# Causal attention on Trainium2: the diagonal mask added by VectorE in place of two identity products on TensorE

## What is computed

```python
q = (x @ Wq).reshape(b, t, HKV, G, HD)
k = (x @ Wk).reshape(b, t, HKV, HD)
v = (x @ Wv).reshape(b, t, HKV, HD)
scores = jnp.einsum('bqhgd,bkhd->bhgqk', q, k) / jnp.sqrt(jnp.float32(HD))
causal = jnp.tril(jnp.ones((t, t), bool))
scores = jnp.where(causal, scores, NEG)
attn = jax.nn.softmax(scores, axis=-1)
ctx = jnp.einsum('bhgqk,bkhd->bqhgd', attn, v).reshape(b, t, HQ * HD)
return ctx @ Wo
```

## Time and profile before

| what | value |
|---|---|
| median of 3 runs | 1102.44 us (1102.1, 1102.44, 1114.94) |
| the profiled execution's own time | 1114.54 us |
| its span, first to last instruction | 1112.8 us |
| mean granted TensorE clock | 0.901 |
| busy over the span: TensorE / weight load / VectorE / ScalarE / GpSimd | 87% / 45% / 70% / 56% / 41% |
| causal attention, items 0 to 127 | from 566 to about 900 us |

### The profile page before, as it was taken

One profiled execution on the slowest core, in us unless ns is written; L12 is line 12 of the kernel. 1 busy time (PEld: TensorE's weight loads), 2 busy tenths in 40 slices (PEclk: granted clock), 3 DMA queues, 4 the chain that ended last, 5 costly groups with the idle time before them and its releaser, 6 DMA issues. The chain is left out here.

```text
span 1112.8 us, 21185 instructions
## 1 busy us (share of the span) xinstructions
PE 964.5 (87%) x6168; PEld 501.9 (45%) x6168; DVE 779.8 (70%) x1622; ACT 624.5 (56%) x1540; POOL 459.8 (41%) x696
## 2 busy tenths in 40 slices
PE   3679999999999986999789999999999968855493
PEld 1212223333333233666445655655555545644393
DVE  7788999999999957566636656666665658735252
ACT  4638888888888872222275566556656623411162
POOL 4222544544544552000235545544545536742452
PEclk9559999999999996799899999999999987855697
DMA  3010000000000000000100000000000000007354
GB/s 83 7 27 6 1 2 2 1 0 0 0 0 0 0 1 1 7 15 22 38 8 16 8 9 14 7 7 14 7 7 9 1 1 0 1 22 157 93 173 132
DMA packets 45227, 24.96 MB, mean 22 GB/s; under 512 B 11976, under 2 KB 43520, under 8 KB 45168
## 3 DMA queue, kind: packets, MB, share of 16 engines
q1 hardware_dynamic: 43920, 21.66, 7.7%
q0 software_dynamic: 1248, 2.57, 0.7%
HBM read 19.08 MB, written 5.15 MB: 22 GB/s over the span
## 5 line engine op out<-in xcount | busy, mean ns | idle before, releaser
L645 DVE TENSOR_REDUCE a_nmax<-a_rows 128x2 f32<-128x1024 f32 x256 | 299.0, 1217 | 14.9 <-PE a_rows L487 11.5
L784 ACT ACTIVATE a_probs<-a_turned 128x512 f32<-128x512 f32 x512 | 269.6, 603 | 44.1 <-PE a_turned L509 42.5
L1212 POOL TENSOR_TENSOR a_prob<-a_prob,a_rinv 128x256 f32<-128x256 f32 (+3 forms) x128 | 159.9, 1254 | 173.1 <-DVE a_rinv L1402 172.8
L1395 DVE TENSOR_REDUCE a_nmax<-a_score 128x2 f32<-128x256 f32 (+3 forms) x128 | 105.5, 824 | 125.2 <-PE a_score L1251 121.1
L1349 ACT ACTIVATE a_prob<-a_score,a_nmax 128x128 f32<-128x128 f32 (+3 forms) x256 | 132.7, 523 | 82.5 <-DVE a_nmax L1395 81.3
L509 PE MATMUL a_turned<-a_q,a_qk 32*128 32x512 bf16 x512 | 137.8, 392 | 5.7 <-ACT a_probs L784 4.0
L472 PE MATMUL a_acc<-a_probs,a_vg 128*32 128x512 f32 x1024 | 139.4, 617 | 0.8 <-ACT a_probs L784 0.7
L487 PE MATMUL a_rows<-a_qk 32*128 32x512 bf16 x512 | 111.9, 402 | 13.4 <-DVE a_nmax L645 6.1
L1248 PE MATMUL a_score<-a_k_s,a_q_s 64*128 64x384 f32 (+3 forms) x512 | 103.6, 481 | 2.2 <-ACT a_prob L1349 1.3
L509 PEld LDWEIGHTS a_turned<-a_q,a_qk 32*128 32x128 bf16 x512 | 35.1, 91 | 152.9 <-ACT a_probs L784 129.0
L1408 DVE COPY a_pt<-a_turn 128x128 f32<-128x128 f32 (+3 forms) x224 | 92.1, 447 | 1.4 <-PE a_turn L1262 1.4
(11 more groups left out here) (314 smaller groups left out, 1623.1 us busy)
## 6 DMA issues: line engine op xcount, KB each, us to landing
m_w<-L_ffn_w SPq DMA_DIRECT2D x23, 256.0 KB
a_wq<-L_attn_Wq SPq DMA_DIRECT2D x16, 128.0 KB, 2.2
m_w_all<-L_ffn_w SPq DMA_DIRECT2D x4, 512.0 KB, 11.7
xs_sorted<-m_blank SPq DMA_DIRECT2D x1, 1495.0 KB, 12.1
m_xs<-xs_sorted SPq DMA_DIRECT2D x5, 260.0 KB, 4.5
g_X<-x SPq DMA_DIRECT2D x4, 256.0 KB, 3.5
g_m_wgu<-L_ffn_gate_up_proj SPq DMA_DIRECT2D x8, 128.0 KB, 2.1
a_wk<-L_attn_Wk SPq DMA_DIRECT2D x32, 32.0 KB, 2.0
```

What stands on the lines that cost most here:

```text
L645: dve.tensor_reduce(nmax[i % 2][:, p // 2, (p % 2) * 2:(p % 2) * 2 + 2], rows[n % 2][:, :, :], AX_X, ALU.max, negate=True).then_inc(row_ou ...
L784: act.activation(probs[:, (tb % 2) * 4 + j, :], turned[n % 3][:, :], ACT.Exp, scale=float(HD0) ** -0.5).then_inc(turn_out, 1)
L1212: pool.tensor_tensor(pr, pr, spread(rinv[:, t % RING, :], 2, width), ALU.mult).then_inc(scl, 1)
L1395: dve.tensor_reduce(nmax[:, t % RING, :], score[t % 2][:, :, 0:width], AX_X, ALU.max, negate=True).then_inc(mx, 1)
```

## The change

`causal` becomes an fp32 tile. TensorE no longer adds it: the score products close their accumulation themselves, and the second one raises `s_s`. VectorE, after its wait for `s_s`, adds `causal` in place to the last 128 columns of both heads in the score tile (one instruction of 128x256 elements, `causal` read twice), waits for a new semaphore `msk` until that has landed, and then takes the maxima. The wait for the finished `causal` tile goes from TensorE to VectorE.

```diff
-        causal = sc.sb("causal", [P, P], BF16)
+        causal = sc.sb("causal", [P, P])
...
+        msk = sc.sem("masked")
...
             pe.wait_ge(v_ev, NT)
-            pe.wait_ge(cz, 2)
...
                 for j in range(2):
                     h = slice(HD1 * j, HD1 * j + HD1)
-                    pe.matmul(score[t % 2][:, j, 0:width], q_s[i % 2][p][h, sb * P:(sb + 1) * P],
-                              k_s[i % 2][h, 0:width], start=True, stop=False)
-                for j in range(2):
-                    last = pe.matmul(score[t % 2][:, j, sb * P:width], g.ident16[:, :], causal[:, :],
-                                     start=False, stop=True)
+                    last = pe.matmul(score[t % 2][:, j, 0:width], q_s[i % 2][p][h, sb * P:(sb + 1) * P],
+                                     k_s[i % 2][h, 0:width], start=True, stop=True)
                 last.then_inc(s_s, 1)
...
             ln.vector_norm(dve)
+            dve.wait_ge(cz, 2)
 
             def max_of(i, r, it):
                 t, width = ITEMS * i + it, (BLOCKS[it % SB] + 1) * P
+                diag = score[t % 2][:, :, width - P:width]
                 dve.wait_ge(s_s, t + 1 + 2 * ITEMS * r)
+                dve.tensor_tensor(diag, diag, spread(causal[:, :], 1, 2), ALU.add).then_inc(msk, 1)
+                dve.wait_ge(msk, t + 1 + 2 * ITEMS * r)
                 dve.tensor_reduce(nmax[:, t % RING, :], score[t % 2][:, :, 0:width], AX_X, ALU.max,
                                   negate=True).then_inc(mx, 1)
```

## The result

Slower by 0.7%: the ratio of the changed kernel to the kernel before is 1.0068, 95% interval 1.0047 to 1.0089. The median of 20 runs is 1118.45 us (1113.41 to 1121.92); the kernel before, run 20 times beside it, has 1111.81 us (1102.1 to 1114.94), and not the 1102.44 us of its first three runs. The profiled execution took 1117.51 us, span 1115.8 us, against 1114.54 and 1112.8. The forecast was 1104.4 us, range 1090 to 1118, a change of +2 us; on 1111.81 us the ratio is +7.6 us (5.2 to 9.9). That it would be slower, and by less than 2%, came out; the size did not, and the median lies just above the range.

A forecast was written before the change was run, and what follows sets the result against it. TensorE's issue was taken as the bound: 1.015 us of new waits against 0.96 saved, +0.06 us a unit, +1 us over 16, another 1 us at the ends; +2 on the 1102.44 median gives 1104.4 us, range 1090 to 1118.

The forecast's parts named there:

- TensorE's issue is the bound: Causal stage: TensorE's pieces follow without gaps, 21.10 us a unit of eight items, 16 units about 338 us.
- A pair costs 0.12 us: Each removed pair of mask products saves TensorE 0.12 us, 0.96 a unit; 0.22 was weighed as the other price.
- The chain through the maximum is 0.245 us longer: From the score products' start: add and maximum's start cost 0.455 us, less 0.21 because scores are ready sooner.
- The dear add: Rival: the in-place accumulator add takes more than 0.42 us, each further 0.1 us costing 6.4 us in all; chance 0.18.
- The four places: Places in a unit where TensorE would newly wait behind VectorE's longer chain, 1.015 us a unit in sum.
- (a): Items 1 and 5: transposes wait for the first half's copy; slack 0.21, a wait of 0.275 us twice a unit.
- (c): Item 7: the next query projection waits for ScalarE's key copy; slack 0.20, a wait of 0.285 us.
- (d): Item 0 of the next unit waits for the query copy; slack 0, a wait of 0.08 us.
- (b): Item 3: the second half's transposes wait for the second copy; slack 0.39, a wait of 0.10 us once a unit.
- The sign that it named: 128-column scores to item 1's six transposes stay within 0.1 of 1.84 us although two pairs are gone.
- The first unit and the way out cost 1 us more: In the first unit and at the last item's way out the chain counts fully: another 1 us.
- The clock falls: Rival: TensorE waiting 5% of the stage lowers its granted clock, at 0.95 up to +17 us; chance 0.04.

The follow-up runs named there:

- run 20: Not a label but part of "run 20 times beside it": the unchanged kernel before, run 20 times beside the changed one; median 1111.81 us.
- no_mask: The changed kernel without the add, so no score is masked; 20.46 us a unit, ratio to the kernel before 0.9858.
- act_copy_both: act_copy_order with ScalarE also copying the second transposed tile of items 3 and 7; 20.46 us a unit, ratio to the kernel before 0.9921.
- act_copy: The changed kernel with ScalarE also copying the first transposed tile of items 1 and 5; 20.95 us a unit, ratio to the kernel before 0.9969.
- order_only: The changed kernel with ScalarE's key copy between item 6's exponentials and query copy ahead of item 7's; 21.17 us a unit, ratio to the kernel before 1.0009.
- both: The kernel before, mask products kept, plus an in-place VectorE add of a tile of zeros; 22.47 us a unit, ratio to the kernel before 1.0200.
- before_order: The kernel before, mask on TensorE, with the extra ScalarE copy and moved projection copies of act_copy_order; 21.06 us a unit, ratio 0.9954.
- act_copy_order: The changed kernel with the extra ScalarE copy of act_copy and the moved projection copies of order_only; 20.57 us a unit, ratio to the kernel before 0.9919.
- half_add: The changed kernel with the add on the first head's diagonal block only, 128x128; 21.05 us a unit, ratio to the kernel before 0.9980.

## Why the prediction was right or wrong

*TensorE's issue is the bound, VectorE's and ScalarE's waits are not free room: right.* no_mask and act_copy_both end at the same 20.46 us a unit, one with none and one with 55 us of adds in the stage, so only the chains matter and not VectorE's load.

*A pair costs 0.12 us: wrong, 0.07 to 0.08 by no_mask.* I read the distance to the next start and left out that the transposes behind the pair would grow by 0.05 us. Of the two prices that I weighed, 0.12 and 0.22, the larger is refuted; what part a change of tiling mode has in either no run shows. By itself this step cost the forecast less than it seems, since, as I wrote, inside the four windows the chain sets the end: with 0.08 my own sums give waits of 0.195 twice, 0.02, 0.205 and 0.12, together 0.74, and a unit of 20.46 + 0.74 = 21.20, against 21.16 in the forecast.

*The chain through the maximum is 0.245 us longer: right within 0.02.* The add was 0.433 and not 0.42, the maximum behind it 0.47 and not 0.455. From the start of item 0's scores to the end of the first copy the chain took 1.57 us before (709.58 to 711.15) and takes 1.83 now (708.22 to 710.05): 0.26 longer. The dear add, the rival that ended slower, did not happen, and the 65 ns for the accumulator that the Trainium skill, VectorE: DVE Perf Modes, led me to weigh did not show: 0.433 us less 0.267 for the elements leaves 0.166, beside 0.14 with the output elsewhere.

*The four places: right, each shown by a run that takes it away.* act_copy removes (a) and nothing else, order_only removes (c) and (d), and act_copy_both, against act_copy_order, removes (b).

*How long TensorE waits at them: this is the step that failed.* Measured, the waits are 21.56 - 20.46 = 1.10 us a unit, 0.36 over the 0.74 above. In the prediction's terms: the slacks of the sum were too large. It let TensorE see the end of a copy after 0.06 us and then start at once, everywhere. The sign that it named shows the miss: from the 128-column scores to the six transposes it is 1.98 us (708.22 to 710.20) and not within 0.1 of 1.84.

At (a) TensorE starts 0.15 us after the copy's end (copy from 709.64 for 0.41, transposes at 710.20). The 0.06 of the prediction is right at item 0, where the scores start that long after ScalarE's query copy. The kernel before has both times, for the same copy and the same products, one in a unit of the hardware loop and one in a unit that is written out:

```profile
814.43 0.59 ACT L1338 ACTIVATE a_q_s<-a_misc 128x512 f32<-128x512 f32 x1
815.08 0.49 PE L1248 MATMUL a_score<-a_k_s,a_q_s 64*128 64x128 f32 x4
...
835.53 0.59 ACT L1338 ACTIVATE a_q_s<-a_misc 128x512 f32<-128x512 f32 x1
836.27 0.49 PE L1248 MATMUL a_score<-a_k_s,a_q_s 64*128 64x128 f32 x4
```

To the nanosecond it is 0.053 and 0.145 us from the end of the copy to the first product. So it is not ScalarE or VectorE that makes the difference. The packed trace also records semaphore instructions, which the views above leave out, and they go with it. In the loop the weight load itself carries the wait for the query copy. In the written-out units, and at (a), where two waits stand ahead of the transposes, the wait for the copy is an instruction of its own (EVENT_SEMAPHORE): it starts 0.04 us after the copy's end, the weight load 0.12 after it, the product 0.15. At (b) the load carries the wait again, and the transpose starts 0.055 us after VectorE's copy. All traces looked at agree in this; no run changes the form of a wait alone.

At (b) the cost lies one step further. In the changed kernel:

```profile
714.21 0.67 DVE L1409 COPY a_pt<-a_turn 128x512 f32<-128x512 f32 x1
...
714.76 0.50 PE L1259 MATMUL a_turn<-g_ident,a_prob 128*128 128x128 f32 x2
715.27 2.38 PE L1272 MATMUL a_acc<-a_pt,a_v_s 128*64 128x512 f32 x16
```

The second transpose starts at 714.94, hardly late. But the value products, with several waits ahead of them, start 0.30 us behind it (0.33 in this unit) where act_copy_both has 0.20.

Place by place, the change of each stretch of a unit (the middle over the stage) against the forecast one:

| place | forecast | measured | what made the difference |
|---|---|---|---|
| (a), twice | +0.035 each | +0.15 each | start 0.09 later, chain 0.015 longer, transposes 0.02 longer |
| (b) | -0.14 | -0.04 | value products 0.10 later behind the second transpose |
| (c) and (d) | +0.125 | +0.19 | the projection behind the wait takes 1.06 us and not 0.95; (d) hides a part |

In sum a unit grew by 0.45 us and not by 0.06. At (c) the wait itself came as forecast, 4.28 us from item 6's scores to the projection (700.52 to 704.80) where the sum gave 4.265. That all waits together, 1.10 us, lie near the 1.015 of the prediction is luck: the pair's price of 0.12 made them too long in the sum by about as much as the slacks made them too short.

*The first unit and the way out cost 1 us more: about right.* Together they grew by 0.84 + 0.4 us, where 0.12 and the 1 us were forecast.

*The time in us: the difference was put on 1102.44.* That was the median of three runs, two of which were among the fastest of 20; the profiled execution at 1114.54 was nearer to the usual. With +7 in place of +2 the same base gives 1109, with the right base and +2 it is 1114: it took both errors to leave the range. I had the row that warned of it, 12 us between the profile and the median, and widened the range but not the middle.

*The clock falls: did not happen.* It reads 1.00 in the stage in the changed kernel, and also in the kernel named both, where the waits are longest.

*Open.* Outside the stage the eleven traces differ by more than the kernels do. The first score products come at 561.3 to 566.5 us, and from the last residual add to the end of the span it takes 195.3 to 205.8 us; 205.4 in before, 195.7 in before_order, with the granted clock between 910 and 990 us at 0.74 and 0.84:

```profile
910.00:990.00 80.00, 65.43 (x302) 47.37 (x301) 53.38 (x113) 25.72 (x44) 48.33 (x46) 0.74 0.00 1
```

```profile
910.00:990.00 80.00, 55.51 (x296) 38.46 (x296) 57.57 (x139) 25.50 (x44) 53.68 (x56) 0.84 0.01 2
```

The first row is of before, the second of before_order. No instruction differs there. This spread is enough for the runs of before to lie between 1102 and 1115 us. The runs without a profile fit this: before_order has a mean granted clock of 0.918 (the middle of 11 runs), the kernel before beside it 0.908 (25 runs). A straight line through the 25 gives 4.7 us for 0.01 of the mean clock, and at equal clock before_order is 1.0 us shorter, as its stage is. By the same line act_copy_order is 7.4 us shorter than the kernel before, and its stage 7.6: the 9 us of its ratio hold some 2 that are not the stage's. The line is rough: for order_only it gives 4.0 us more than before, and the stage 1.5. Whether the order of work in the stage changes how often the tail runs at the higher clock, or chance did, was not tried.

## What to carry to other kernels

Work taken from a full engine and put on one with gaps is free only if no chain through the second engine comes back to the first with less slack than the work is long: list the places where the full engine waits for a result behind the moved work, and take the slack of each from start times, less the time that the engine takes to start again after a wait. Read that time at a place whose wait has the same form: here it was 0.05 us where the weight load carries the wait and 0.15 where the wait is an instruction of its own. Then look for what stands on that queue, or on another engine's, for no reason: here three copies, moved into gaps of ScalarE, turned a loss of 0.7% into a gain of 0.8%, while the same moves gave the stage of the kernel before only 0.9 us. A short product between two large ones may be worth less than its distance to the next start; its price is known only from a run without it.

## What the runs showed that was not expected

- A mask pair of 0.12 us from start to start was worth 0.07 to 0.08 us when removed; in every item the transposes behind it took 0.05 us longer.
- TensorE starts 0.053 us after the end of the copy that it waits for where its weight load carries the wait, and 0.145 us after it where the wait is an instruction of its own, behind ScalarE's copies and VectorE's alike (in half_add the copy ended at 710.95, and the load began at 711.07, the product at 711.10). After a wait for ScalarE's key copy the projection starts 0.05 us after the end and then takes 0.10 us longer.
- An in-place fp32 add of 128x256 in the accumulator takes 433 ns, 25 ns more than the row of the same size with its output elsewhere; one of 128x128 takes 300 ns, beside 0.29 us elsewhere.
- Between half_add and the changed kernel, each 0.1 us on VectorE's chain costs 0.4 us a unit, since four chains of a unit pass through it.
